# Attention inner loop: the context transposes split over two steps, VectorE's reciprocal and the maxima transpose at other steps

## The reference, cut to what matters

```python
Xn = (X - mu) * rsqrt(var + LN_EPS) * ln_w + ln_b
Q, K, V = split(einsum('bsd,df->bsf', Xn, W_in))   # 16 heads of 16 channels, S = 1024
Q, K = (_rope(Q), _rope(K))
scores = einsum('bhqd,bhkd->bhqk', Q, K) / sqrt(16)
probs = softmax(scores, axis=-1)
ctx = einsum('bhqk,bhkd->bhqd', probs, V)          # then times W_out, as one row per token
```

## Time and profile before

| what | value |
|---|---|
| median of 3 runs | 1094.04 us (1091.96 to 1095.35) |
| the profiled execution | 1091.91 us, its span 1090.1 us |
| PE busy, share of the span | 1028.6 us, 94% |
| PEld, DVE, ACT, POOL busy | 814.3, 791.0, 674.2, 507.2 us |
| granted TensorE clock, mean | 0.982 |
| steps n = 3 to 15 of the attention | about 66.9 to 213.7 us from the span's start |

### The profile page before, as it was taken

One profiled execution on the slowest core, in us unless ns is written; L12 is line 12 of the kernel. 1 busy time (PEld: TensorE's weight loads), 2 busy tenths in 40 slices (PEclk: granted clock), 3 DMA queues, 4 the chain that ended last, 5 costly groups with the idle time before them and its releaser, 6 DMA issues. The chain is left out here.

```text
span 1090.1 us, 18619 instructions
## 1 busy us (share of the span) xinstructions
PE 1028.6 (94%) x6437; PEld 814.3 (75%) x6437; DVE 791.0 (73%) x1789; ACT 674.2 (62%) x1235; POOL 507.2 (47%) x457
## 2 busy tenths in 40 slices
PE   7999999989999998699999999999889999999997
PEld 5433333347788987689988999899789878888997
DVE  5788998837656856899899999998667555333843
ACT  4478888756644346778777887788556344333454
POOL 3252321114047661677777676767606000536644
PEclk9999999989999998899999999999899999999999
DMA  3534434105214300352122221220010123654200
GB/s 92 89 64 58 73 49 72 41 24 172 87 43 147 63 1 8 114 184 73 54 64 78 93 64 54 80 81 31 15 36 26 45 58 85 159 157 141 90 20 20
DMA packets 80633, 79.28 MB, mean 73 GB/s; under 512 B 29320, under 2 KB 67676, under 8 KB 80540
## 3 DMA queue, kind: packets, MB, share of 16 engines
q1 hardware_dynamic: 80228, 77.66, 26.9%
q10 hardware_dynamic: 312, 0.43, 0.3%
HBM read 65.51 MB, written 1.28 MB: 61 GB/s over the span
## 5 line engine op out<-in xcount | busy, mean ns | idle before, releaser
L672 ACT ACTIVATE attn_probs<-attn_rows_k 128x512 f32<-128x512 f32 x256 | 133.8, 598 | 37.6 <-PE attn_rows_k L524 37.4
L760 DVE TENSOR_REDUCE attn_row_max<-s_sum 128x1 f32<-128x512 f32 x171 | 111.3, 681 | 17.1 <-PE s_sum L510 16.0
L524 PE MATMUL attn_rows_k<-attn_q_stack,attn_k_stack 50*128 50x512 f32 x256 | 94.2, 457 | 9.2 <-ACT attn_probs L672 9.2
L2872 DVE TENSOR_TENSOR late_mids<-late_mids,late_bank 128x512 f32<-128x512 f32 (+1 forms) x50 | 34.4, 687 | 78.7 <-PE late_bank L67 75.7
L65 PE MATMUL late_bank<-net_x_part_low,late_w_T 128*128 128x512 f32 (+1 forms) x192 | 77.9, 406 | 0.0
L66 PE MATMUL late_bank<-net_x_part_low,late_w_T 128*128 128x512 f32 (+1 forms) x192 | 76.1, 396 | 0.0
L67 PE MATMUL late_bank<-net_x_part_low,late_w_T 128*128 128x512 f32 (+1 forms) x192 | 76.0, 396 | 0.0
L1537 POOL TENSOR_TENSOR gold_mids<-gold_mids,gold_weight 128x512 f32<-128x512 f32 x32 | 51.9, 1659 | 48.6 <-DMA gold_weight<-gold_weights 48.6
L510 PE MATMUL s_sum<-attn_k_stack,attn_q_stack 48*128 48x512 f32 x171 | 72.6, 468 | 1.7 <-DMA attn_q_stack<-s_part 1.3
L2777 ACT ACTIVATE late_mids<-late_bank 128x512 f32<-128x512 f32 (+1 forms) x50 | 29.9, 597 | 69.6 <-PE late_bank L67 69.6
L2973 POOL TENSOR_TENSOR late_mids<-late_mids,late_raw_w_T_last 128x512 f32<-128x512 f32 x22 | 30.0, 1384 | 88.6 <-DMA late_raw_w_T_last<-top_weights 88.6
(11 more groups left out here) (459 smaller groups left out, 3532.1 us busy)
## 6 DMA issues: line engine op xcount, KB each, us to landing
lin_mix<-decay_sums SPq DMA_DIRECT2D x16, 512.0 KB, 3.9
lin_q_dec<-decay_sums SPq DMA_DIRECT2D x16, 512.0 KB, 5.3
gold_weight<-gold_weights SPq DMA_DIRECT2D x16, 256.0 KB, 3.5
attn_k_stack<-s_part SPq DMA_DIRECT2D x30, 128.0 KB, 3.6
s_raw_ring<-in_L_ffn_Wg SPq DMA_DIRECT2D x12, 256.0 KB, 2.8
s_raw_ring<-in_L_ffn_Wu SPq DMA_DIRECT2D x12, 256.0 KB, 3.2
attn_q_stack<-s_part SPq DMA_DIRECT2D x32, 64.0 KB, 2.4
gold_raw_w_down<-in_L_ffn_Wd SPq DMA_DIRECT2D x1, 2048.0 KB, 12.9
```

The costliest lines, as they stand in the source:

```text
L524: pe.matmul(ps_k[n % 3][:, :], k_stack[rows, h % SLOTS, t * P:(t + 1) * P], q_stack[rows, h % SLOTS, :], start=True, stop=True).then_inc(s ...
L672: act.activation(probs[:, kk % PB, side * HALF:(side + 1) * HALF], ps_k[n % 3][:, :], ACT.Exp)\
L760: dve.tensor_reduce(row_max[:, tile, half:half + 1], ps_q[n % 3][:, :], axis=AX, op=ALU.max)\
```

## The change

`turn_ctx` is given a half: pieces 0 and 1 at u = 4, pieces 2 and 3 at u = 6, both between pair 3 and pair 4, with the waits only before the first. The semaphore `ctx_turned` counts two per head. `take_ctx` follows at u = 6. `turn_max` moves from before pair 3 to between pair 3 and pair 4 of u = 2. The reciprocal `norm_ctx(n - 3)` at u = 7 becomes `norm_ctx(n - 4)` at u = 3, which is the same head's reciprocal four units later.

```diff
-        U_MAX, U_CTX, U_NORM, U_COPY = 2, 4, 7, 7
+        U_MAX, U_CTX, U_TAKE, U_NORM, U_COPY = 2, (4, 6), 6, 3, 7
...
-                def turn_ctx(h):
-                    pe.wait_ge(ctx_copied, h + 1)
-                    if h + 3 <= NH:
-                        pe.wait_ge(max_copied, h + 3)
-                    else:
-                        pe.wait_ge(ctx_taken, h)
-                    for c in range(4):
+                def turn_ctx(h, half):
+                    if half == 0:
+                        pe.wait_ge(ctx_copied, h + 1)
+                        if h + 3 <= NH:
+                            pe.wait_ge(max_copied, h + 3)
+                        else:
+                            pe.wait_ge(ctx_taken, h)
+                    for c in (2 * half, 2 * half + 1):
...
-                    if u == U_MAX and 1 <= n <= NH:
-                        turn_max(n - 1)
                     if g is not None:
                         score_rows_q(g, 0)
                     if kk is not None:
                         score_rows_k(kk, 1)
-                    if u == U_CTX and 3 <= n:
-                        turn_ctx(n - 3)
+                    if u == U_MAX and 1 <= n <= NH:
+                        turn_max(n - 1)
+                    if u in U_CTX and 3 <= n:
+                        turn_ctx(n - 3, U_CTX.index(u))
...
-                turn_ctx(NH - 1)
+                for half in range(2):
+                    turn_ctx(NH - 1, half)
...
-                        act.wait_ge(ctx_turned, h - 1)
+                        act.wait_ge(ctx_turned, 2 * (h - 1))
...
-                    act.wait_ge(ctx_turned, h + 1)
+                    act.wait_ge(ctx_turned, 2 * (h + 1))
...
-                    if u == U_CTX and 3 <= n:
+                    if u == U_TAKE and 3 <= n:
                         take_ctx(n - 3)
...
-                    if u == U_NORM and 3 <= n < NH:
-                        norm_ctx(n - 3)
+                    if u == U_NORM and 4 <= n <= NH:
+                        norm_ctx(n - 4)
```

## The result

The changed kernel takes 1100.24 us, median of 20 executions (1093.80 to 1105.66), beside 1094.83 (1091.96 to 1101.35, 20 executions) for the kernel before on the same chip. I had forecast 1093.8 with a range of 1090.3 to 1096.3 and most of the chance on "within 0.3%". Two later measurements of the same changed kernel gave +7.0 and +4.9 us over before. The executions spread: of the 36 of the changed kernel in the three measurements 22 took over 1098 us, of the 168 of the kernel before beside all runs 18 did, and the fastest of the changed kernel (1093.80) lies where the typical one of before does.

What follows compares the result with a forecast made beforehand. No engine was solid, so the order of waits was taken to bound the kernel. Terms -2.7, -0.8, +1.6, +0.4 and +1.3 summed to -0.2: 1091.7 us profiled, median 1093.8, range 1090.3 to 1096.3.

Steps and rivals of the forecast that it cites:

- What bounds it: Attention's steady part: order of waits decides; a head takes 11.29 us, 0.49 over four bare groups, in groups A and B.
- Splitting: Context transposes in two halves, in groups B and C: B falls to 2.70 us, C stays; -2.7 us over 13 steps.
- The smaller price of a transpose: Weight loads between pairs 3 and 4: about 0.105 us each from the trace, against the skill's about 275 ns.
- Rival 2: Transpose halves overshoot the 0.70 us gap between pairs 3 and 4; with 0.1 overshoot +2.4, 1096.4 us; chance 0.10.
- The reciprocal out of A, `turn_max` behind pair 3: Group A: -0.15 us per step without the reciprocal, +0.04 for the moved maxima's turn; -0.8 us in all.
- GpSimd late: Preparation queued behind the later reciprocal delays the maxima's split and TensorE at three heads; +1.6 us, bounds 0 and +3.
- Rival 1: GpSimd hands over in time, so its stall vanishes: -2.3 us, 1091.8, or 1090.4 with other bounds; chance 0.24.
- The reciprocal's new place: VectorE before group C's pair 3: 0.12 us added against about 0.08 in hand; +0.4 us over 12 groups, bounds 0 and 1.4.
- Rival 3: VectorE binds everywhere, so the time freed in B becomes a wait for the last maximum: +1.8 us, 1095.8; chance 0.08.
- `take_ctx`: ScalarE in group C, directly before `copy_ctx`: may delay D's first exponential by 0.08 us; costed at nothing, 1.0 without cover.
- The end: Steps n = 16 and 17, where TensorE itself binds and changeovers cost in full: +1.3 us, bounds 0.3 and 1.8.
- up to some 3 us: Error allowed if steps before n = 3 have a longer clock dip near 54 to 56 us, or none.

Runs made afterwards that it cites:

- the filled best version: Changed kernel, weighing last, maxima's turn back before pair 3, context halves joined in steps 16-17, dummy matmuls in units 12-15 and at end: 1088.29, again 1091.46 us.

## Why the prediction was wrong, point by point

**What bounds it.** Right: the period of a head went from 11.29 to 10.99 in steps without a preparation, by 0.21 in B and 0.13 in A, less 0.04 in D.

**Splitting.** Right, -2.8 for -2.7. The smaller price of a transpose held: two loads take 0.20. But I had misread the figure against it. Each of the 64 transposes is recorded at 0.27 us (at most 0.33) before and after, so this trace agrees with the about 275 ns for one that the prediction takes from the Trainium skill, "TensorE: Matmul & The Clock Gate", "Part 4: PE-mode transpose"; in a row they overlap and start 0.11 apart (0.17 behind the first), and that is what a gap has to hold. Rival 2 (halves don't fit) is out; pair 4 waits for the exponential.

**The reciprocal out of A, `turn_max` behind pair 3.** Right, -1.04 for -0.8.

**GpSimd late.** Mechanism right, at the three steps named, and its lateness right to 0.06 us; the term was mis-sized, +2.55 for +1.6. The wait itself was 0.75 in the head where nothing else happened (3.59 against 2.84), for 0.60. And I did not cost that the merge would now meet GpSimd's last operation, which held VectorE for 1.07 us in two of three heads and made their group A another 0.32 longer; one more merge was held, at 216.61, and cost nothing: group A of n = 16 is 3.07 with it, and 3.07 with the maxima's turn alone, where no merge was held. Rival 1 (GpSimd in time) is out, and putting the weighing last takes back 2.8 of the stretch.

**The reciprocal's new place.** +0.05 for +0.4: the margin in C must be larger than the 0.08 that I read; where, I have not measured. Rival 3 (VectorE binds everywhere) is out.

**`take_ctx`.** +0.45 for nothing. I had named the price without cover, 1.0; about half of it came.

**The end.** Right, +1.31 for +1.3.

So the sum was off by 0.7 us: +0.5 where I had -0.2. With it the forecast would have been 1094.5, inside the range, while 1100.24 was measured. Another 0.8 is the base, 1094.04 from three executions where twenty gave 1094.83; that leaves about 4.9. **The step that failed is the one behind the sum**: "All later blocks start after this one's end and shift with it", with the median moved by the loop's sum alone. The later blocks do not only shift. From the next block's first matmul to the end the two profiles of before take 851.8 and 850.5 us, the three of the changed kernel 859.4, 856.6 and 857.0, over the same instructions, with a further fall of 10.2 us right behind the block. I had seen one such stretch and allowed "up to some 3 us" for the steps before n = 3 only, and for the blocks behind nothing.

How much of the median's +5.4 is clock? Over 148 executions of the kernel before, the time falls by 0.66 us for each 0.001 of mean granted clock (a straight line through time and clock; 1093.6 at 0.980). The 36 executions of the changed kernel have a mean clock of 0.9734 and a mean time of 1099.8; before has 0.9778 and 1095.0. Of these 4.8 us the line gives 0.0044 / 0.001 x 0.66 = 2.9 to the clock, the loop accounts for 0.5, and 1.4 remain. The line for the changed kernel's own 20 executions is steeper (0.90 per 0.001), by which the clock would take 4.0 and the rest would be nothing to speak of; the division is no sharper than that.

**What is shown**: the loop's +0.5 and its parts; that the changed kernel runs at a lower mean clock; that in the profiles of both kernels the stretches at half clock lie outside the loop (in one of the fifteen other profiles one lies inside); that the changed kernel loses time behind the block, where its three profiles have a second fall, and that such a fall goes with about 5 us; that work which changes nothing in the loop's stretch moves the median by -8.4 (fill at units 12 to 15; -4 to -8 by the ratios) or by more than its length (1.35 us at the end of the loop). **What is argued and not shown**: that the changed kernel's loss comes from the place of the block's end against the falls. For it: before with its end moved by 0.45 to 1.35 us loses 0.8 to 5.6, and then 22 of 48 executions take over 1098 us, as 22 of 36 of the changed kernel do, against 18 of 168; changed with 0.9 more does not lose further, as far as the noise lets one see. Against it, or not fitted: the profiled executions of before with a later end lay in the lower part of their kernels' times (1092.3 to 1095.1) and had no second fall, so I have not seen in a profile where their loss lies; and the last `weigh` alone does not sort the table above, since 234.79 has the second fall and 234.55, 236.24 and 239.58 have none. A rival is not excluded: that it is the maxima's turn behind pair 3, and not the end's place. Of the five profiles with the second fall four have it there (the changed kernel's three and the turn alone, whose median rose by 1.8), and of the nine without dummy matmuls whose turn stands ahead of pair 3 none has the fall. Against it: the changed kernel with the weighing last has the turn behind pair 3, no second fall and a median 0.5 below before, and the filled best version has the fall with the turn ahead. The changed kernel with the turn alone put back was not run. Why the fill at units 12 to 15 also removed the second fall, 200 us later, stays open too, and so does the fall near 803 us. The Trainium skill, "TensorE: Matmul & The Clock Gate", "Part 1: The HAM clock gate", says that the gate watches activity on a timing of its own that runs freely of the kernel, so that the same kernel meets it in different phases; the executions of one kernel here do differ that way (17.1 and 6.8 us near 53 us in the same code), but no run here isolates it.

## What to carry to other kernels

Cost an in-order engine's queue to the end, as was done here for GpSimd, and then ask what else runs at the new time: here a merge on VectorE with two SBUF inputs that landed behind the start of a GpSimd operation waited for its end. Where a profile has stretches at half clock, a sum of durations bounds only the changed stretch; the median can move by ten times that sum, so the range has to hold one or two such stretches (here some 5 us for one of 10.2) at either side, and two kernels should be compared by the stretch between marks as well as by the median. Parts that are priced one by one in such a stretch can be recombined: the two that gain with the queue mended and without the two that lose gave 0.32%, and 0.4 to 0.5% with TensorE's pauses filled (not clearly more).

## What the runs showed of the hardware that I had not expected

- The merge of 128x8 values takes 0.17 us, and 1.04 to 1.24 when GpSimd's 1.27 us operation is already running on SBUF operands; a reduction of a PSUM piece that runs beside GpSimd's sum of two SBUF operands keeps its 0.69 (93.88).
- 0.45, 0.9 and 1.35 us of added TensorE work before the block's end cost 0.8 to 2.3, 3.2 and 5.6 us, of which the last is clear of the noise by far and the first is not.
- A transpose of 128x128 f32 is recorded at 0.27 us, and in a row they start 0.11 to 0.17 apart.
- Twelve dummy score matmuls in pauses of TensorE took out a stretch at half clock of 7 to 17 us and made the changed kernel 8.4 us faster than its six executions beside it (4 to 8 by the ratios); in the kernel before, with twelve more at the end, they were worth 1.1 us, within the noise.
